# Second attention: rotated sums rounded straight into the operands of the scores, by GpSimd and ScalarE, with no transfers of rounded sums

## The reference

```python
kv_c = _linear(x, d_kv_w, d_kv_b)                       # 64 latent values per token
k_c = _linear(kv_c, u_k_w, u_k_b).reshape(b, s, H, Dh)
k_r = _linear(kv_c, qr_w, qr_b).reshape(b, s, H, Dr)
v = _linear(kv_c, u_v_w, u_v_b).reshape(b, s, H, Dh)
q_c_lat = _linear(x, d_q_w, d_q_b)
q_c = _linear(q_c_lat, u_q_w, u_q_b).reshape(b, s, H, Dh)
q_r = _linear(q_c_lat, qr_w, qr_b).reshape(b, s, H, Dr)
q_r, k_r = _rope(q_r), _rope(k_r)
scores = jnp.einsum('bqhd,bkhd->bhqk', q, k) * scale    # q, k: content and rotated values joined
probs = jax.nn.softmax(scores, axis=-1)
ctx = jnp.einsum('bhqk,bkhd->bqhd', probs, v).reshape(b, s, H * Dh)
return _linear(ctx, out_w, out_b)
```

## Time and profile before

| | us |
|---|---|
| three timed runs | 2585.75, 2583.29, 2586.13 |
| median | 2585.75 |
| profiled execution, its own time | 2584.44 |
| its span in the profile | 2583.1 |

### The profile page before, as it was taken

The page is one execution under the profiler, slowest core; times in us unless marked ns, Lnnn a source line. Parts: engine busy times, 40 slices in busy tenths (PEclk is TensorE's granted clock), DMA queues, the critical chain, the costliest instruction groups (busy, mean ns, idle before and its releaser), DMA issues.

```text
span 2583.1 us, 50515 instructions
## 1 busy us (share of the span) xinstructions
PE 2243.7 (87%) x18441; PEld 1587.8 (61%) x18528; DVE 2116.8 (82%) x3186; ACT 1826.6 (71%) x2575; POOL 931.9 (36%) x1424
## 2 busy tenths in 40 slices
PE   5888888869986699989899999989999999988899
PEld 2444444435554366767667777767766766766587
DVE  6888888678885499899899899899899898888522
ACT  4777777727675388888788888888788787777411
POOL 3321122102222364553554554545545545422200
PEclk9999999969998699999999999999999999999899
DMA  3000000050000399999999999999999999999200
GB/s 123 1 2 2 2 2 2 1 111 1 1 1 1 55 196 198 196 193 201 188 198 194 200 197 200 195 197 198 194 197 201 193 200 196 202 193 195 57 17 17
DMA packets 1129557, 317.46 MB, mean 123 GB/s; under 512 B 1109280, under 2 KB 1118464, under 8 KB 1128448
## 3 DMA queue, kind: packets, MB, share of 16 engines
q1 hardware_dynamic: 1126464, 312.00, 68.6%
q10 hardware_dynamic: 2848, 2.23, 0.3%
HBM read 18.45 MB, written 2.10 MB: 8 GB/s over the span
## 4 chain that ended last, share of the span: by engine, by line
DVE 21%; PE 20%; DMA 11%; issue 7%; ACT 6%; SPq 2%; POOL 0%; DVEq 0%; ACTq 0%; POOLq 0%
DMA partsT<-parts 11%; DVE parts L1540 10%; DVE lows L1524 9%; PE psS L1471 3%; PE psOb L1391 3%; PE psS L1374 2%; ACT prob L1691 2%; ACT q_hi L1673 2%; PE psS L1375 1%; PE psS L1376 1%; PE psOb L1392 1%; ACT parts L1701 1%; PE psOb L1427 1%; PE psOb L1491 1%; PE psPb L1491 1%
## 5 line engine op out<-in xcount | busy, mean ns | idle before, releaser
L1691 ACT ACTIVATE prob<-psS,shift 128x1024 f32<-128x1024 f32 x512 | 574.0, 1121 | 160.6 <-DVE shift L1532 155.5
L1540 DVE TENSOR_TENSOR parts<-prob,parts 128x1024 f16<-128x1024 f32 x512 | 628.0, 1227 | 20.1 <-ACT parts L1701 17.0
L1524 DVE TENSOR_REDUCE lows<-psS 128x1 f32<-128x1024 f32 x512 | 623.1, 1217 | 12.1 <-PE psS L1376 9.6
L1701 ACT CAST parts<-prob 128x1024 f16<-128x1024 f32 x512 | 538.6, 1052 | 75.4 <-DMA partsT<-parts 70.2
L1374 PE MATMUL psS<-k_hi,q_lo 128*128 128x512 f32 x1024 | 441.8, 431 | 87.2 <-ACT prob L1691 81.6
L1391 PE MATMUL psOb<-kv,partsT 128*128 128x130 f16 x4096 | 405.9, 222 | 60.1 <-DMA partsT<-parts 59.4
L1391 PEld LDWEIGHTS psOb<-kv,partsT 128*128 128x128 f16 x4096 | 357.4, 97 | 138.4 <-DMA partsT<-parts 70.6
L1375 PE MATMUL psS<-k_lo,q_hi 128*128 128x512 f32 x1024 | 404.0, 395 | 0.0
L1376 PE MATMUL psS<-k_hi,q_hi 128*128 128x512 f32 x1024 | 403.2, 394 | 0.0
L1392 PE MATMUL psOb<-kv,partsT 128*128 128x66 f16 x4096 | 394.0, 193 | 0.0
L1392 PEld LDWEIGHTS psOb<-kv,partsT 128*128 128x128 f16 x4096 | 361.7, 98 | 1.0 <-issue 1.0
(11 more groups left out here) (269 smaller groups left out, 3812.6 us busy)
## 6 DMA issues: line engine op xcount, KB each, us to landing
q_hi<-rounded SPq DMA_DIRECT2D x64, 128.0 KB, 3.0
k_hi<-rounded SPq DMA_DIRECT2D x64, 128.0 KB, 2.8
partsT<-parts SPq DMA_TRANSPOSE x512, 4.9
ef<-in_ewT SPq DMA_DIRECT2D x1, 2048.0 KB, 10.9
rf<-in_rwT SPq DMA_DIRECT2D x1, 2048.0 KB, 10.2
outw_s<-in_outwT SPq DMA_DIRECT2D x1, 2048.0 KB, 8.7
trig<-in_trig SPq DMA_DIRECT2D x2, 1024.0 KB, 11.5
out_x<-ot SPq DMA_DIRECT2D x16, 128.0 KB, 1.7
```

What stands on the lines that cost most here:

```text
L1524: dve.tensor_reduce(lows[:, n % 2, g:g + 1], psS[:, (2 * n + g) % 3, :], AX_X, ALU.min).then_inc(half_min, 1)
L1540: dve.tensor_tensor(parts[:, s, 1, :], prob[:, g, :], parts[:, s, 0, :], ALU.subtract).then_inc(low_done, 1)
L1691: act.activation(prob[:, g, :], psS[:, (2 * n + g) % 3, :], ACT.Exp, bias=shift[:, n % 2:n % 2 + 1], scale=-1.0).then_inc(exp_done, 1)
L1701: act.copy(parts[:, s, 0, :], prob[:, g, :]).then_inc(high_done, 1)
```

## The change

`rounded` and the two transfers are gone. GpSimd adds queries and keys apart, two instructions of 64 partitions in the place of one of 128. The keys' sum reads the `latent` rows of `rot0` and `rot1` and writes the `rotary` rows of a new tile `whole_k`. ScalarE rounds each sum straight into `q_hi` and `k_hi`, two instructions of 64 partitions: the queries' where the one rounding stood, the keys' one tile later (tiles 4, 7, 10 and 13), again between the second exponential and the second high part. The rests are subtracted as before, from the new places. TensorE's wait for `moved` at the first score of a head goes, and ScalarE's and SyncE's too.

```diff
-            def round_sums(head, j):
-                c = 4 * head + j
-                act.wait_ge(added_up, c + 1)
-                if c:
-                    act.wait_ge(rests_done, 2 * c)
-                    act.wait_ge(moved, 32 * c)
-                act.copy(rounded[:, :], whole[:, :]).then_inc(round_done, 1)
+            def round_queries(head, j, halves_scored):
+                act.wait_ge(added_up, 2 * (4 * head + j) + 1)
+                if halves_scored:
+                    act.wait_ge(score_ready, halves_scored)
+                act.copy(q_hi[rotary, q_slot(head, j), :], whole[rotary, :]).then_inc(round_done, 1)
+
+            def round_keys(head, j):
+                act.wait_ge(added_up, 2 * (4 * head + j) + 2)
+                act.copy(k_hi[head % 2][rotary, j * BANK:(j + 1) * BANK], whole_k[rotary, :]).then_inc(round_done, 1)
...
                 if ahead and n % NT in (3, 6, 9, 12):
-                    round_sums(n // NT + 1, n % NT // 3 - 1)
+                    round_queries(n // NT + 1, n % NT // 3 - 1, 2 * (n + 1))
+                if ahead and n % NT in (4, 7, 10, 13):
+                    round_keys(n // NT + 1, n % NT // 3 - 1)
                 high(n, 1)
...
-                pool.tensor_tensor(whole[:, :], rot[0][:, :], rot[1][:, :], ALU.add).then_inc(added_up, 1)
-                pool.wait_ge(added_up, c + 1)
+                for side, (out_rows, rows) in enumerate(((whole, rotary), (whole_k, latent))):
+                    pool.tensor_tensor(out_rows[rotary, :], rot[0][rows, :], rot[1][rows, :], ALU.add).then_inc(added_up, 1)
+                    pool.wait_ge(added_up, 2 * c + side + 1)
...
-                if n < TILES and n // NT + 1 < NH and n % NT in (3, 6, 9, 12):
-                    move_sums(n // NT + 1, n % NT // 3 - 1, 2 * (n + 1))
                 turn_contexts(n - 4)
```

More of the change, by code:

```diff
@@ L1226, in second_attention @@
         whole = sb(L, "whole", [P, BANK])
-        rounded = sb(L, "rounded", [P, BANK], F32R)
+        whole_k = sb(L, "whole_k", [P, BANK])
         prob = sb(L, "prob", [P, 2, HB])
@@ L1240, in second_attention @@
         piece_ready, rotated, added_up = sem("b_piece"), sem("b_rotated"), sem("b_added_up")
-        round_done, rests_done, moved = sem("b_round"), sem("b_rests"), sem("b_moved")
+        round_done, rests_done = sem("b_round"), sem("b_rests")
         folded, rested = sem("b_folded"), sem("b_rested")
@@ L1368, in scores @@
                     pe.wait_ge(rests_done, 8 * (head + 1))
-                    pe.wait_ge(moved, 128 * (head + 1))
                     pe.wait_ge(rested, 4 * (head + 1))
@@ L1506, in rotate @@
                 if 4 * head + j:
-                    dve.wait_ge(added_up, 4 * head + j)
+                    dve.wait_ge(added_up, 2 * (4 * head + j))
                 dve.scalar_tensor_tensor(out=rot[kind][:, :], in0=psP[:, :], scalar=br[kind][:, head:head + 1],
@@ L1741, in scalar @@
                 fold(0, piece, 0)
-                round_sums(0, piece // 3)
+                round_queries(0, piece // 3, 0)
+                round_keys(0, piece // 3)
             for n in range(TILES + 3):
@@ L1798, in add_up @@
                     pool.wait_ge(rests_done, 2 * c)
-                pool.tensor_tensor(whole[:, :], rot[0][:, :], rot[1][:, :], ALU.add).then_inc(added_up, 1)
-                pool.wait_ge(added_up, c + 1)
+                for side, (out_rows, rows) in enumerate(((whole, rotary), (whole_k, latent))):
+                    pool.tensor_tensor(out_rows[rotary, :], rot[0][rows, :], rot[1][rows, :], ALU.add).then_inc(added_up, 1)
+                    pool.wait_ge(added_up, 2 * c + side + 1)
             def rest_queries(head, j, halves_scored):
                 slot = q_slot(head, j)
-                pool.wait_ge(round_done, 4 * head + j + 1)
+                pool.wait_ge(round_done, 2 * (4 * head + j) + 1)
                 if halves_scored:
                     pool.wait_ge(score_ready, halves_scored)
-                pool.tensor_tensor(q_lo[rotary, slot, :], whole[rotary, :], rounded[rotary, :].bitcast(F32),
+                pool.tensor_tensor(q_lo[rotary, slot, :], whole[rotary, :], q_hi[rotary, slot, :].bitcast(F32),
                                    ALU.subtract).then_inc(rests_done, 1)
@@ L1811, in rest_keys @@
             def rest_keys(head, j):
-                pool.wait_ge(round_done, 4 * head + j + 1)
-                pool.tensor_tensor(k_lo[head % 2][rotary, j * BANK:(j + 1) * BANK], whole[latent, :],
-                                   rounded[latent, :].bitcast(F32), ALU.subtract).then_inc(rests_done, 1)
+                cols = slice(j * BANK, (j + 1) * BANK)
+                pool.wait_ge(round_done, 2 * (4 * head + j) + 2)
+                pool.tensor_tensor(k_lo[head % 2][rotary, cols], whole_k[rotary, :], k_hi[head % 2][rotary, cols].bitcast(F32),
+                                   ALU.subtract).then_inc(rests_done, 1)
                 pool.wait_ge(rests_done, 8 * head + 2 * j + 2)
@@ L1893, in turn_probabilities @@
                                        parts[:, s, :, :].rearrange("p a k -> p (a k)")).then_inc(landed[s], 16)
[L1895 to L1901, removed]
             def turn_contexts(n):
@@ L1931, in load_down @@
                 sp.dma_start(wdn[:, :, :], wdownT.rearrange("(k p) n -> p k n", p=P)).then_inc(down_loaded, 16)
-            for j in range(NB):
-                move_sums(0, j, 0)
             for n in range(TILES + 4):
```

## The result

The changed kernel takes 2541.99 us (median of four executions, 2537.88 to 2545.20) against 2585.15 of the kernel before (median of four, 2583.29 to 2586.13): a ratio of 0.9834, 95% interval 0.9821 to 0.9846. The prediction said 2554, range 2530 to 2582, and faster. The side and the mechanism were right; the gain is 43 us where 32 were forecast. The profiled execution is the fastest of the four (2537.88 us, span 2536.6). A second profiled execution of the same kernel has the same loop (heads 1 to 13 in 1188.2 us) and a span of 2540.8: it enters the loop 3.9 us later (886.2 against 882.3), so I read the change in the loop, by heads.

The account below looks back on a forecast made before the run. The prediction took the transfer-issuing queue as the bound (93.8 of 94.15 us a head), VectorE next at 87.3. Gross gain 49 minus costs of 17 gave net 32 us: 2554 us, range 2530 to 2582.

Parts of the forecast that it names:

- The rival that the queue isn't the limit: Issuing queue has real idle time, so heads 1 to 13 keep 94.15 us: 2570 to 2590 us, chance 0.18.
- The gross gain of 49: Removing the moves from the issuing queue: 42 us of VectorE waits in heads 1 to 13, plus heads 14 and 15.
- The fold's term: VectorE's 36.2 us wait for ScalarE's fold, over 52 places in heads 1 to 13: 24 us stay, 12 go.
- Left-over lateness of the queue, 5 us: Queue still held 87.4 of some 91 us a head: a cost of 0.4 us in each of 13 heads.
- part 1: The pairs of moves leave the issuing queue, 6.4 us a head; gross gain forecast 49 us.
- Head 14, 15 and 0: Gains outside heads 1 to 13: 6 us in head 14, 1 in head 15, nothing in head 0.
- Part 2: The same work on other engines, GpSimd's second sum and ScalarE's extra rounding: costs of 2, 6.5 and 3.5 us.
- ScalarE's rounding in tile 13: In heads with outputs the extra rounding delays the high part, for which VectorE's low part already waits: 2 us.
- The second sum at the port: GpSimd's second sum overlaps VectorE's low part in tiles 2, 5, 8, 11: 34 places of 0.19, 6.5 us.
- The slipped addition in tile 12: In odd heads, the later split pushes GpSimd's addition to x into a low part: 3.5 us.
- The rival of more freed: The fold's remaining waits fall by half and the queue's left-overs vanish: about 2537 us, chance 0.13 for below 2540.
- The rival of the slow port: GpSimd runs later, so its second sum holds the low part longer, up to 1.09 us: at most 2619, chance 0.06.

Follow-up runs that it names:

- kernel with the moves gone: Kernel before with the pairs of moves taken out of heads 1 to 14 and nothing put in their place: 2536.85 us, ratio 0.9815.
- the sum cut short: Changed kernel with GpSimd's second sum (the keys' rotated part) cut to 32 of 512 columns from head 1 on: 2535.01 us, ratio 0.9815.
- the fold first: Changed kernel with TensorE projecting the folded piece ahead of an earlier tile's output and VectorE taking its rest ahead of the reciprocal: 2538.83 us, ratio 0.9827.

## Why the prediction was right, and where its sizes were off

**The bound: right.** The budget of the queue (93.8 us of 94.15) named what limits, and putting the moves back alone costs the 43 us again. The rival that the queue isn't the limit has fallen. Two of the proofs offered for it were weaker than they looked. Rows that join without a gap can't show a full queue, since the joined rows of the changed kernel hide 128.3 us of gaps; that those of before hide only 12.8 was not known. And head 0, where budget and time agreed within 0.2 us, was no proof: without its moves it takes 90.7 us, not less, and even before the queue had 5.2 us of gaps there. By the Trainium skill (DMA: Bandwidth & Descriptors, "Issuing engines are not separate DMA queues") the time saved on an issuing sequencer is usually small relative to the transfer. These runs differ where it is one queue that is full: with next to no data the issues alone cost 31 us on SyncE and nothing on ScalarE. With the other statement of this section of the Trainium skill, that all transfers run on the same sixteen engines whoever issues them, the runs agree: the full moves on ScalarE cost 66 us.

**The gross gain of 49: right in the sum, and in most of its terms.** Measured 48. By terms, heads 1 to 13, kernel with the moves gone against the earlier trace rows: reciprocals 21.8 forecast, 21.2 measured; low parts 3.4, 1.6; rotations 5, 5.8; fold 12, 7.9. That is 36.5 where 42 were forecast. The fold's term failed by a count: it left 24 us and 28.3 stayed. The estimate of 0.8 us for a wait behind an output was right (0.83 in tiles 2, 5 and 8 of even heads), but tile 11 of odd heads waits 0.85 too, since outputs have begun by then, and the sum had it at 0.28: 7 x 0.57 = 4.0 us. These waits stay because ScalarE waits for the piece from TensorE (47.0 us over 52 pieces in these heads, 52.7 before) and not for the queue. Most of the 5.5 us that are missing was made up elsewhere. VectorE's busy time fell by 4.1 us (1135.16 to 1131.06), though its instructions last as long as before: an instruction that doesn't wait starts while the one ahead ends, as here in the changed kernel, where each row begins some 0.08 us before the last is over:

```profile
1558.94 0.15 DVE L1549 RECIPROCAL rden<-psOb 128x1 f32<-128x1 f32 x1
1559.01 0.73 DVE L1507 SCALAR_TENSOR_TENSOR rot<-psPb,br,trig 128x512 f32<-128x512 f32 x1
1559.66 1.26 DVE L1539 TENSOR_TENSOR parts<-prob,parts 128x1024 f16<-128x1024 f32 x1
```

A wait that goes gives its own time and this overlap, and I had counted none. In these heads 970 instructions start before the one ahead is over where 933 did: 37 more at 0.08 us, 3.1 of the 4.1 us. The other 1 us I can't place.

**Left-over lateness of the queue, 5 us: wrong.** It was charged at 0.4 us a head because the queue would hold 87.4 of 91 us. No reciprocal waits any more and ScalarE waits 0.6 us in thirteen heads. The step that failed is the 87.4: the queue is held for 81.6 us a head, because the issues of the transposes got shorter as it emptied, so it is full to 89% and not to 96%. How much of the remaining unevenness the ring of four halves takes up is not shown; no run varies the ring. Heads 1 to 13 gained 41.2 us from part 1, where the forecast, after this charge, had 37.

**Head 14, 15 and 0: right.** 5.8, 0.9 and -0.7 us against 6, 1 and 0. In heads 14 and 15 the queue is still full after the change: 1.4 and 0.4 us of gaps.

**Part 2, 12 us without that charge: too much; measured 5.** ScalarE's rounding in tile 13 was charged 2 us as a high part that comes late. It acts by another path, through GpSimd's rest of the keys and the port, and makes the low parts of tiles 13 and 14 some 2 us longer in all; but with the sum cut short nothing of part 2's cost is left in the time. The second sum at the port was charged 6.5 us at 34 places of 0.19. It is there, and as large as said: 1.36 us in tile 2 and 1.41 at most other places in place of 1.21 (three take 1.66 to 1.70), against the 1.40 of the forecast. But the places are 27, since tile 11 of odd heads has the long wait: 7 x (0.13 + 0.22 + 0.22) + 6 x 0.24 = 5.4 us (over-runs here counted against the 0.02 of before). The slipped addition in tile 12 (3.5 us) didn't cost anything: it runs 0.12 us into the low part, which still takes 1.21. The exclusive lock of the Trainium skill (SBUF — State Buffer, "SBUF: two separate sides") would have made it the full overlap, 0.28 us in the rows of tile 2 above: the low part was 0.15 us longer than 1.21. The trace agrees on the blocking and hides 0.13 us of it, as the forecast had taken from the earlier trace rows. The same 0.12 to 0.13 is hidden where the overlap is 0.34 (1.43 us, tile 13 above) and 0.62 (1.71 us, the fold first).

The sum of the misses: 4 us on part 1 with its left-overs, 7 on part 2. That is 11 of the 12 us between 2554 and 2542. The sum of part 1 came out as near as it did partly by luck: the waits gave 5.5 us less than forecast, and 4.1 us that nobody had counted came in. The rival of more freed (2537) was nearly as near, but half of its reason isn't so: the left-overs vanished, as it said, while the waits of the fold did not shrink by half. The rival of the slow port fell: the over-runs average 0.26 us at most in any of those tiles.

**The tests named ahead.** Heads 1 to 13 at 91 to 92.5: 91.4. VectorE busy 87.5 to 88: 87.5. Reciprocals under 6 us: 0.2. ScalarE's wait under 15: 0.6. Low parts of 1.40 in tiles 2, 5, 8 and 11 of odd heads: yes, but tile 11 in even ones. Gaps in the issuing queue: yes, 128.3 us of them, though only issue by issue, since the timeline joins the rows.

## What to carry to other kernels

Add up what one issuing queue is held for in a period of the loop and set it beside the period: when they agree, a small transfer costs its place in the queue whatever it carries, and the view of waits can hide that. Don't trust a joined row for the sum: read the issues one by one, and pair each with the instruction that it waits for; how late it begins behind it says whether the queue limits. Moving the transfer to another engine's queue isn't the remedy if its bytes then run beside the ones that matter; having a computing engine write the value where it is wanted is. When the wait that bound the loop is gone, the next limit may be a port: look where the added instruction ends relative to the instruction that it can hold, and expect that moving it moves the hold.

## What the runs showed of the hardware that I had not expected

A pair of transfers of one row of 64 bytes each costs on SyncE's queue most of what a pair of 64 rows and 128 KB each does (0.59 against 0.77 us of run time). The same full pairs issued from ScalarE's queue stretch the issue of the next transpose on SyncE's to 4.0 us at the median, where it is 2.8 with 1/32 of the bytes, and cost 1.3 us a pair; with 1/32 of the bytes they cost nothing. The issue of a transpose isn't a fixed time either: 2.52 us in the mean on the full queue, 2.40 once it had gaps. And on VectorE a wait costs some 0.08 us beyond its length, in lost overlap with the instruction ahead.
